# Late additions in the seventh chunk, the last gated tile on DVE, and four smaller moves in a two-layer kernel

## The reference

```
x = ln(x + time_mix(x, Wk, Wv, Wr, Wo, decay, first))      # RWKV: sigmoid(r) * (num / (den + 1e-6)), then Wo
x = ln(x + feed_forward(x))       # fwht, up and gate (2048 each), silu(gate) * up, fwht, down
x = ln(x + attention(x))          # 16 heads of 32, rope, causal softmax over 512 tokens, output projection
x = ln(x + shared(x) + routed(x)) # one shared expert (352 wide, fp32), top 2 of 8 experts in bf16
```

## Time and profile before

| | us |
|---|---|
| median of 3 runs | 1560.73 (1559.9 to 1564.29) |
| the profiled execution | 1560.44 |
| its span, first to last instruction | 1558.7 |
| PE busy in it | 1477.2 (95%) |
| DVE, ACT, POOL busy | 985.1, 613.7, 475.2 |
| mean granted clock of PE | 0.984 of full speed |

### The profile page before, as it was taken

How to read it: one execution, slowest core, us unless ns; L and a number is a source line. 1 busy time by engine, 2 the same in 40 slices (tenths; PEclk the granted TensorE clock), 3 DMA queues, 4 the chain that set the end, 5 groups by cost and what they waited for, 6 DMA issues and landing times. The chain is left out here.

```text
span 1558.7 us, 22522 instructions
## 1 busy us (share of the span) xinstructions
PE 1477.2 (95%) x7682; PEld 1076.1 (69%) x7696; DVE 985.1 (63%) x1906; ACT 613.7 (39%) x1085; POOL 475.2 (30%) x377
## 2 busy tenths in 40 slices
PE   7999899999999999999999999999999899997996
PEld 6788678788888888888887764444444377774554
DVE  6878987845545554553432767777777375566664
ACT  5243355613412431441211135554555636331554
POOL 1233433303411440441342222222222265004760
PEclk9999999999999999999999989999999999998999
DMA  6022347404311430424257683566662656821336
GB/s 216 28 82 85 131 147 254 177 3 148 94 54 53 149 94 0 132 83 164 99 189 236 196 219 110 175 178 188 196 188 101 237 201 214 321 110 52 105 97 229
DMA packets 105228, 223.39 MB, mean 143 GB/s; under 512 B 9328, under 2 KB 35312, under 8 KB 104240
## 3 DMA queue, kind: packets, MB, share of 16 engines
q1 hardware_dynamic: 101392, 211.96, 41.8%
q0 software_dynamic: 3744, 10.23, 2.1%
HBM read 157.54 MB, written 64.36 MB: 142 GB/s over the span
## 5 line engine op out<-in xcount | busy, mean ns | idle before, releaser
L1992 ACT ACTIVATE at_pt<-at_st 128x512 f32<-128x512 f32 (+3 forms) x384 | 164.1, 497 | 147.1 <-PE at_st L2024 146.3
L958 POOL TENSOR_TENSOR ff_w_lo<-ff_raw,ff_w_hi 128x1024 fp32r<-128x1024 f32 x64 | 155.4, 2429 | 205.4 <-ACT ff_w_hi L988 205.4
L115 PE MATMUL op_bank<-ff_x_hi,ff_w_lo 128*128 128x512 f32 x512 | 199.3, 389 | 0.0
L117 PE MATMUL op_bank<-ff_x_hi,ff_w_hi 128*128 128x512 f32 x512 | 199.3, 389 | 0.0
L116 PE MATMUL op_bank<-ff_x_lo,ff_w_hi 128*128 128x512 f32 x512 | 199.2, 389 | 0.0
L1225 DVE TENSOR_TENSOR ff_h_lo<-ff_hf,ff_h_hi 128x512 f32 (+1 forms) x64 | 148.2, 2315 | 53.8 <-ACT ff_h_hi L1113 53.5
L2024 PE MATMUL at_st<-mx_qp,mx_kp 98*128 98x512 f32 (+3 forms) x288 | 103.4, 391 | 13.9 <-ACT at_pt L1992 10.7
L988 ACT ACTIVATE ff_w_hi<-ff_raw 128x1024 fp32r<-128x1024 f32 x64 | 67.8, 1061 | 118.4 <-PE op_bank L117 116.1
L115 PEld LDWEIGHTS op_bank<-ff_x_hi,ff_w_lo 128*128 128x128 f32 x512 | 96.1, 188 | 20.2
L117 PEld LDWEIGHTS op_bank<-ff_x_hi,ff_w_hi 128*128 128x128 f32 x512 | 96.1, 188 | 20.0
L116 PEld LDWEIGHTS op_bank<-ff_x_lo,ff_w_hi 128*128 128x128 f32 x512 | 96.1, 188 | 20.0
(11 more groups left out here) (453 smaller groups left out, 3345.9 us busy)
## 6 DMA issues: line engine op xcount, KB each, us to landing
ff_raw<-in_Wug SPq DMA_DIRECT2D x64, 512.0 KB, 3.6
at_raw<-in_expert_gu SPq DMA_DIRECT2D x16, 704.0 KB, 12.3
mx_qp<-q_hi SPq DMA_DIRECT2D x12, 512.0 KB, 6.4
mx_kp<-k_hi SPq DMA_DIRECT2D x12, 512.0 KB, 11.2
at_raw<-in_expert_d SPq DMA_DIRECT2D x8, 768.0 KB, 13.9
expert_gu_bf<-at_cast SPq DMA_DIRECT2D x16, 352.0 KB, 10.9
ex_e_gu<-expert_gu_bf SPq DMA_DIRECT2D x8, 704.0 KB, 8.6
tm_ln_res<-in_x SPq DMA_DIRECT2D x4, 1024.0 KB, 5.4
```

The source lines that it names most:

```text
L115: pe.matmul(out, cut_l(ll), cut_r(rh), start=first, stop=False, **kw)
L117: return pe.matmul(out, cut_l(lh), cut_r(rh), start=False, stop=last, **kw)
L958: pool.tensor_tensor(w[j][1][:, :, :, :], raw[:, j], f32(w[j][0][:, :, :, :]), ALU.subtract)\
L1992: act.activation(pt[:, s % PT, h, off:TB], st[(s * HG + h) % ST][:, off:TB], ACT.Exp, scale=SCALE).then_inc(exp_done, 1)
```

## The change

Six edits.

1. The product and the subtraction of the last gated tile of time mix (block 3, tile 3) go from POOL to DVE. DVE does the product ahead of the butterflies and the subtraction between their two levels.
2. `add_late` of the last two tiles goes from DVE's steps 0 and 1 to 6 and 7, `root_late` on POOL from step 2 to 7, `scale_late` on ACT from steps 0 and 3 to 6 and 8 (for block 2 and block 3), and SP's two stores from behind the issue of chunks 4 and 7 to behind that of chunks 8 and 10.
3. Maxima pieces use the bank one further, and PE's wait for the negated maxima goes from piece 0 to the last of the first round of banks.
4. The high part of the output projection's weights is cast by POOL, in unit 6 behind the experts' casts, instead of by ACT in unit 7.
5. PE's wait for the ones of attention goes from ahead of the loop to the first weighted sum.
6. `turn` of parts 2 and 3 stands behind steps 2 and 3 instead of 1 and 2.

```diff
@@ on_gpsimd of time mix
-            for m in range(1, KT):
+            for m in range(1, KT if i < NB - 1 else KT - 1):
                 gate(i, m)
@@ on_vector of time mix
-        ff.fly_steps(dve, 0)
+        s, j, m = NB * KT - 1, (KT - 1) % 2, KT - 1
+        dve.wait_ge(rec_ready, s + 1)
+        dve.wait_ge(rw_ready, s)
+        dve.tensor_tensor(rw[:, j, :], num[:, j, :], rec[:, j, :], ALU.mult).then_inc(rw_ready, 1)
+        ff.fly_steps(dve, 0, (0,))
+        dve.wait_ge(rw_hi_ready, s + 1)
+        dve.wait_ge(rw_lo_ready, s)
+        dve.tensor_tensor(rw_lo[:, (NB - 1) % 2, m, :], rw[:, j, :], f32(rw_hi[:, (NB - 1) % 2, m, :]), ALU.subtract)\
+            .then_inc(rw_lo_ready, 1)
+        ff.fly_steps(dve, 0, (1,))
@@ first_block on SP
                 chunk(sp, 0, n - n % 2, n % 2)
-                if n in (4, 7):
-                    tm.ln.store(sp, NB - 2 if n == 4 else NB - 1)
+                if n in (8, 10):
+                    tm.ln.store(sp, NB - 2 if n == 8 else NB - 1)
@@ feed-forward on POOL, ACT and DVE
-                    if folding(i) and n + j == 2:
+                    if folding(i) and n + j == 7:
                         tm.root_late(pool)
...
-                        if n + j in (0, 3):
-                            tm.scale_late(act, NB - 1 if n + j else NB - 2)
+                        if n + j in (6, 8):
+                            tm.scale_late(act, NB - 2 if n + j == 6 else NB - 1)
...
-                        if n + j < 2:
-                            tm.add_late(dve, 2 + n + j)
+                        if n + j in (6, 7):
+                            tm.add_late(dve, n + j - 4)
@@ piece on PE (and the same bank in its reading on DVE)
-        bank = self.bank[n % len(self.bank)]
-        if n == 0:
+        bank = self.bank[(n + 1) % len(self.bank)]
+        if n == len(self.bank) - 1:
             at_least(pe, self.neg_hi_ready, u)
             at_least(pe, self.neg_lo_ready, u)
+        if n == 0:
             pe.wait_ge(self.loaded[j], (c + 1) * self.LOADS * DMA)
@@ high of the output weights
-    def high(self, act):
-        act.wait_ge(self.loaded, DMA)
-        act.activation(self.w[0][:, :, :], self.raw[:, :, :], ACT.Copy).then_inc(self.hi_ready, 1)
+    def high(self, pool):
+        pool.wait_ge(self.loaded, DMA)
+        pool.tensor_copy(self.w[0][:, :, :], self.raw[:, :, :]).then_inc(self.hi_ready, 1)
@@ attention on POOL, ACT and PE
+                        if u == UNITS - 2:
+                            ow.high(pool)
...
-                    if s == OW_STEP:
-                        ow.high(act)
...
                     mx.wait_v(pe, u)
+                    pe.wait_ge(ones_small_set, 1)
...
-            pe.wait_ge(ones_small_set, 1)
@@ after_last on PE
-            if i < NB - 1 and k in (1, 2):
-                turn(i + 1, k + 1)
+            if i < NB - 1 and k in (2, 3):
+                turn(i + 1, k)
```

More of the change, by code:

```diff
@@ L1016, in mix, with fly_steps @@
         pe.matmul(aux[m % 2][:, :], had_r[:, :], z_hi[:, m, :], start=False, stop=True).then_inc(aux_done, 1)
-    def fly_steps(dve, i):
+    def fly_steps(dve, i, levels=(0, 1)):
         assert KT == 4
-        dve.wait_ge(signed, (i + 1) * KT)
-        for lev in range(2):
+        if 0 in levels:
+            dve.wait_ge(signed, (i + 1) * KT)
+        for lev in levels:
             src, dst = (fly[(lev + n) % 2][:, :, :].rearrange("p (g two e) n -> p g two e n", two=2, e=1 << lev)
@@ L1366, in top @@
         out = self.tops[:, h, qt:qt + 1] if lo == 0 else self.tops2[:, h, qt - TT:qt - TT + 1]
-        piece = self.bank[n % len(self.bank)][:, 0:hi - lo]
+        piece = self.bank[(n + 1) % len(self.bank)][:, 0:hi - lo]
         if hi == (qt + 1) * P:
```

## The result

The changed kernel takes 1572.79 us (median of 5 runs, 1571.9 to 1574.88); the kernel before, in the runs taken beside it and earlier, 1563.19 (5 runs). The ratio is 1.0079, with a 95% interval of 1.0059 to 1.0099: slower by 12.3 us, between 9.2 and 15.5; the two medians above lie 9.6 us apart, at the lower end of that. The forecast was 10 us more, 1571, in a range of 1557 to 1578. The profiled span grew from 1558.7 to 1573.2 us, by 14.5.

The account below looks back on a forecast made before the run. PE was taken as the bound, busy 1477.2 of 1558.7 us. Terms 17.0 + 0.5 + 0 - 4.6 - 0.1 - 2.7 = +10.1 gave 1571 us on the median, range 1557 to 1578.

Parts of the forecast that it names:

- The late additions: Feed-forward block 0: SP stands at stores awaiting later scales, so chunks 9 to 11 come late; +17.0 us, bounds +7.3 and +24.
- the chain: Feed-forward block 0, times of stores, loads and casts: chunk 9 late by 3.1 us, 10 by some 6.5, 11 by 16.3.
- The gain in the first chunks: First feed-forward chunks: additions moved off DVE shorten PE's waits of 2.38 and 1.03 us; 2.7 us gained, bound 3.4.
- The clock: Behind the third stall in feed-forward block 0: a stretch at lower clock that no later wait hides; 3.4 us added once.
- The last gated tile: End of time mix: DVE and POOL take turns, PE goes on at 185.0; +0.5 us, from -3.4 to +2.5.
- Maxima pieces: Attention units: a later wait takes the place of the 0.60 us wait for negated maxima; 0, at best -3.6 us.
- The wait for the ones: Attention: the wait moves to the first weighted sum, other inputs come with the same barrier; -0.1 us.
- The cast on POOL: Last attention unit: PE's 2.73 us wait falls to 0.8 and the clock stays up; -4.6 us, bounds -1.9 and -5.3.
- Turns: Shared expert's turns: two waits (3.17, 1.57 us) each get six matmuls ahead; -2.7 us, bounds 0 and -4.4.
- The rival on the other side: Feed-forward block 0: SP's stand at the stores is hidden and only gains remain; -9.6 us, 1551; chance 11%.
- Short transfers: Feed-forward block 0: stores do not slow chunks, third delay 10 us instead of 16.3, no slow stretch; +0.4, 1561; chance 15%.
- The clock falls after each stall: Feed-forward block 0: slow stretches also show after the other stalls; 6.8 us more, 1578; chance 12%.

Follow-up runs that it names:

- e1: Changed kernel with SP's two stores behind the issues of chunks 10 and 12 instead of 8 and 10: 1550.22 us, ratio 0.9927 to the kernel before.
- e8: Changed kernel with the two stores issued by ACT, each right behind its scale, instead of by SP: 1553.26 us, ratio 0.9941 to the kernel before.
- e12: Changed kernel with only the second store moved, stores behind chunks 8 and 12: 1560.38 us, ratio 1.0000 to the kernel before.
- e3: Kernel before with only the late additions, roots, scales and stores placed as in the changed kernel: 1579.79 us, ratio 1.0119.
- e4: Kernel before with only the last gated tile's product and subtraction moved to DVE: ratio 1.0011.
- e5: Kernel before with only the high part of the output projection's weights cast by POOL in unit 6: ratio 0.9985.
- e6: Kernel before with only the turns of parts 2 and 3 one step back: ratio 0.9967.
- e7: Kernel before with only maxima pieces one bank further and the negated-maxima wait moved, without the move of the wait for the ones: ratio 0.9995.
- e10: e9 plus late additions, roots and scales in steps 6 to 8, SP's stores behind chunks 10 and 12: 1549.94 us, ratio 0.9927 to the kernel before.
- e9: Kernel before with the output weights' cast on POOL and the turns one step back: 1552.15 us, ratio 0.9941.
- e11: e10 with block 2's scale left in step 0 and its store behind chunk 4: 1551.66 us, ratio 0.9949 to the kernel before.
- e2: Kernel before with only SP's two stores moved behind chunks 8 and 10, scales left in steps 0 and 3: 1564.95 us, ratio 1.0021.

## Why the prediction was right, and where it was off

**The late additions, +17.0 forecast, +20.1 in block 0 of the pair, +17.4 alone.** The mechanism is as the prediction had it: SP came to the stores before their scales, stood, and chunks 9, 10 and 11 came late one after the other. e1, e8 and e12 show it, since each takes away a stand and leaves the scales, roots and additions. The 17.4 is e3 over the long stretch (18.6 timed). Over the long stretch the pair differs by 20.1 as well (177.5 - 157.4), and edit 1 has 1.7 of it (e4). The first stall was forecast as 3.1 us and was 3.9; the stores, chunk loads and casts came within 2.3 us of the chain's times (with the 2.7 us taken off, as it says: chunk 9's issue 252.5 against 253.75, chunk 10's cast 267.4 against 268.84, chunk 11's 280.5 against 282.72). Where the 3.1 us between 17.0 and 20.1 lie:
- The gain in the first chunks was to be 2.7 and was 1.8: of 2.38 and 1.03 us, 1.57 is left. I took DVE's additions for the whole cause of the wait. This is 0.9.
- Chunk 11 took 7.0 us to land, not 6.4. PE began the mix ahead of chunk 11 at 288.81, where 289.5 less 2.7 is 286.8; of these 2.0 us 0.9 are the smaller gain, 0.6 the later start of the whole, and 0.5 are left for this.
- That mix was to take 1.0 us and took 3.75, for PE waited in it a second time for DVE's z_low, 1.56 us, and ran at half clock. The forecast had no such second wait.

```profile
292.56 0.63 PE L115 MATMUL op_bank<-ff_x_hi,ff_w_lo 128*128 128x512 f32 x1
```

- The clock, 3.4 forecast, held, at 3.1. Chunk 11 ran from 292.56 to 299.99, 2.0 us more than the 5.44 of a chunk, and the mix before it lost 1.1 (3.75 less the wait of 1.56 and the usual 1.09).

These make 0.9, 0.5, 1.6 and -0.3; the rest, 0.4, is not traced.

The stretch after the first stall, 262 to 270 at 0.57, was hidden, as the forecast had it: chunk 9 ended 3 us late by it, and PE still had to wait 1.74 us for the fold's z_low. In e12 the clock at the same place averaged 0.79 and that wait was 3.66, and the mix began 96.7 us behind the last reciprocal step, against 97.1 in the changed kernel. The chain left out that the first mix waits for z_low too, since ACT and DVE do its parts only after the late cast of chunk 10. That cost nothing either, as the 8.38 us behind it are set by chunk 11.

**The last gated tile, +0.5 forecast.** The +0.6 in the table is chance, since it was there before the edit could act. Alone the edit costs 1.7 us (e4, 1.0011, and the long stretch), inside the term's bounds. Its ground holds: DVE and POOL take turns, and PE went on at 185.28 for the 185.0 forecast. What was mis-sized is the start of the comparison. The forecast kept the slow stretch of the earlier trace rows on both sides; in e5, e6 and e7 chunk 0 starts 2.2 us earlier than in the profile that it read, and e4 loses 1.2 of that.

**Maxima pieces, 0 forecast**, 0.9995 alone: in the changed kernel the later wait took the place of the one removed, to the tenth of a microsecond. **The wait for the ones, -0.1 forecast:** no run has this edit alone, but PE's wait at the start of attention is 3.10 us in both profiles, so nothing was gained by it there.

**The cast on POOL, -4.6 forecast, about -2 in the pair.** The wait fell from 2.73 to 0.93 as said (0.8). That the clock "should then stay up" held in some executions only. In the changed kernel the two windows at 0.83 lose 10 x 0.17 = 1.7 us each, the 3.4 again, a little later, and e5 and e10 have such windows too; e1, e8, e9, e11 and e12, with the same code there, have none. All six profiled kernels with the cast on ACT (before, e2, e3, e4, e6, e7) have a slow stretch there. So this part of the gain differs from execution to execution, and the timed worth of the edit alone, 2.3 us (0.9985), is anything from 0 to 5.

**Turns, -2.7 forecast, -4.4 in the pair**, 0.9967 alone, some 5 us. The waits shrank by 1.40 and 1.39, as six matmuls should make them; the rest is the half-clock stretch after the first, which I had kept as the outer bound and which did go. Over the 10 us behind that wait the clock averaged 0.83 before and 1.00 in e6; of the six profiled kernels with the long wait five have 0.70 to 0.83 there and one (e7) 1.00, and the eight with the short one all have 1.00.

**The rival on the other side** had the right sum for another kernel: "only gains remain" was 1551, and e1, where the stand is gone, measured 1550.2, by parts that are off both ways (the gate's move, the cast and the turns). What decided between them was the one thing the rival named, whether SP's stand fits in the time by which chunks are loaded ahead. Chunk 9 went out 8.6 us later than in e1, against 3.5 to 6 us of slack. *Short transfers* failed as landings took 5.5 to 7.0 us. *The clock falls after each stall* was right about the clock behind the first stall and the third, but the first cost nothing, and behind the wait of 1.74 us it stayed at full.

That the total came out near (10 forecast, 12.3 timed) is in part luck. In the profiled pair it is 14.5, 4.4 more than the sum: the loss was too small by 3.1 and the cast's gain too large by 2.6, which add, and the turns' gain was too small by 1.7, which cancels some.

## What to carry to other kernels

When a producer is moved later, move the place in the queue of whatever stores its result, by as many steps, and look at what else is in that queue: a store that waits on an engine that runs in order holds every load behind it. Compare the time the queue will stand with the time by which the loads run ahead of their use (here 13 us, of which landing, cast and subtraction need 7 to 9.5). A wait of PE that is removed may give back more than itself, and one that is added may cost more, by the clock that follows it; such a stretch costs nothing where a later wait hides it, as the first one here. Before a term is read off as a difference of two profiles, look whether the difference was already there ahead of the edit, and start the measured part ahead of everything that the edit moves.

## What the runs showed of the hardware

- A two-input DVE operation of 128 x 512 took 0.69 us with POOL idle and 2.71 beside POOL's two-input operation (e4). The Trainium skill (GPSIMD Engine Reference, section Specifications) names the contention; the size, a factor of four on one operation, is the trace's.
- What a wait of PE does to the clock differs between executions of the same instructions. The wait of 3.1 to 3.2 us at the turn was followed by a mean granted clock of 0.70 to 0.83 over 10 us in five profiled executions and by 1.00 in a sixth; the wait of 1.8 us there by 1.00 in all eight. Behind the wait at 214 us the clock held at full in the kernel before (2.38 us) and averaged 0.88 over 14 us in e4 to e7 and e9 (2.67 to 3.29 us).
- POOL cast 128 x 2048 from fp32 in 1.90 us (changed kernel), ACT in 1.91: for this one-input operation the two are alike.
- A 512 KB load of weights landed 3.6 us after its issue in the median of 64, and 6.1 and 7.0 us behind a 1 MB store (253.75 to 259.89, 275.67 to 282.72 in the changed kernel). A store issued just behind the load, or in another engine's queue, slows it as well. Behind the same two 512 KB loads it was 6.0 us without a store (the kernel before), 7.5 with the store 0.5 us behind it (e1) and 8.6 with the store on ACT 0.7 us ahead of it (e8).
